# Routed tiles with the up weights held still: VectorE copies each tile's weights, the tokens move, the second transposes go, and the gate is applied to the output

## The reference

```python
scores = jax.nn.sigmoid(xf @ router_w.T)
_, top_idx = jax.lax.top_k(scores + expert_bias, TOP_K)
mask = jax.nn.one_hot(top_idx, N_EXPERTS, dtype=xf.dtype).sum(axis=-2)
gates = scores * mask
h12 = jnp.einsum('td,ehd->teh', xf, w12)
h1, h2 = jnp.split(h12, 2, axis=-1)
h = jax.nn.silu(h1) * h2 * gates[:, :, None]
routed = jnp.einsum('teh,edh->td', h, w3)
```

## Time and profile before

| | |
|---|---|
| median of 3 executions | 1631.92 us |
| the profiled execution, its own time | 1630.51 us |
| its span, as the profiler saw it | 1628.6 us |
| TensorE (PE) matmuls busy | 1590.7 us, 98% of the span |
| VectorE (DVE) busy | 1181.4 us, 73% |
| ScalarE (ACT) busy | 883.4 us, 54% |
| GpSimd (POOL) busy | 732.2 us, 45% |

### The profile page before, as it was taken

The page is one execution under the profiler, slowest core; times in us unless marked ns, Lnnn a source line. Parts: engine busy times, 40 slices in busy tenths (PEclk is TensorE's granted clock), DMA queues, the critical chain, the costliest instruction groups (busy, mean ns, idle before and its releaser), DMA issues.

```text
span 1628.6 us, 42340 instructions
## 1 busy us (share of the span) xinstructions
PE 1590.7 (98%) x15030; PEld 1071.6 (66%) x15031; DVE 1181.4 (73%) x2544; ACT 883.4 (54%) x1528; POOL 732.2 (45%) x676
## 2 busy tenths in 40 slices
PE   7999999999999999999999999999999999998998
PEld 3665566666656776766556666666656777877576
DVE  7777775666667767768866566666788879888876
ACT  5354543444377767764433334444366676674764
POOL 2342242434246566553333323344245567777343
PEclk9999999999999999999999999999999999999999
DMA  7132233333311211003311123333433022221001
GB/s 266 53 106 86 89 105 95 110 110 110 88 40 27 39 26 26 0 2 101 96 36 36 39 72 111 110 108 103 104 66 52 2 80 74 68 61 42 27 26 52
DMA packets 91303, 115.74 MB, mean 71 GB/s; under 512 B 9424, under 2 KB 76528, under 8 KB 91184
## 3 DMA queue, kind: packets, MB, share of 16 engines
q1 hardware_dynamic: 70832, 71.21, 15.0%
q0 software_dynamic: 20352, 42.88, 9.1%
HBM read 66.14 MB, written 47.90 MB: 70 GB/s over the span
## 4 chain that ended last, share of the span: by engine, by line
PE 83%; DVE 7%; issue 3%; ACT 3%; POOL 2%; DMA 1%; DVEq 0%; SPq 0%; ACTq 0%; POOLq 0%
PE ps L2004 19%; PE ps L2006 19%; PE ps L2005 19%; PE ps L2299 3%; PE ps L2298 3%; PE ps L2248 2%; PE ps L2249 2%; PE ps L2020 2%; PE ps L2220 2%; PE ps L2201 2%; PE ps L2538 2%; PE ps L2572 2%; PE ps L2550 1%; PE ps L2400 1%; POOL expert_x L759 1%
## 5 line engine op out<-in xcount | busy, mean ns | idle before, releaser
L787 POOL DMA_INDIRECT routed<-work x142 | 136.1, 959 | 236.4 <-DVE work L1675 231.3
L2004 PE MATMUL ps<-later_hi,work 128*128 (+1 forms) x632 | 202.8, 321 | 0.8 <-ACT work L1019 0.6
L2005 PE MATMUL ps<-later_lo,work 128*128 (+1 forms) x632 | 202.6, 321 | 0.0
L2006 PE MATMUL ps<-later_hi,work 128*128 (+1 forms) x632 | 202.6, 321 | 0.0
L2004 PE MATMUL ps<-xt_hi,wsh 128*128 128x512 f16 x508 | 192.6, 379 | 1.9 <-DVE work L1546 1.3
L2006 PE MATMUL ps<-xt_hi,wsh 128*128 128x512 f16 x508 | 192.5, 379 | 0.0
L2005 PE MATMUL ps<-xt_lo,wsh 128*128 128x512 f16 x508 | 192.5, 379 | 0.0
L975 ACT ACTIVATE work<-ps 128x512 f32<-128x512 f32 x128 | 76.4, 597 | 168.6 <-PE ps L2006 160.5
L1662 DVE SCALAR_TENSOR_TENSOR work<-ps,work 128x256 f32<-128x256 f32 x142 | 68.8, 484 | 99.9 <-ACT work L1026 94.7
L2004 PE MATMUL ps<-wsh,work 128*128 128x256 f16 x512 | 139.5, 273 | 0.7 <-DVE work L1475 0.6
L2005 PE MATMUL ps<-wsh,work 128*128 128x256 f16 x512 | 139.5, 273 | 0.0
(11 more groups left out here) (277 smaller groups left out, 4288.0 us busy)
## 6 DMA issues: line engine op xcount, KB each, us to landing
work<-expert_x SPq DMA_DIRECT2D x142, 129.0 KB
yg<-in_w_later SPq DMA_DIRECT2D x9, 498.0 KB
w1q<-in_w_later SPq DMA_DIRECT2D x9, 498.0 KB
yg<-in_w SPq DMA_DIRECT2D x16, 256.0 KB
values<-wsh SPq DMA_DIRECT2D x8, 512.0 KB, 3.0
later_hi<-values SPq DMA_DIRECT2D x16, 256.0 KB, 3.6
later_lo<-values SPq DMA_DIRECT2D x16, 256.0 KB, 3.4
out_x<-x SPq DMA_DIRECT2D x8, 512.0 KB, 2.9
```

The lines of the kernel that those rows point to most:

```text
L787: nc.gpsimd.indirect_dma_start(routed[:, :], bass.IndirectOffsetOnAxis(m.homes[:, i:i + 1], 0), m.t_y[:, i % 4, :], None).then_inc(s[f"til ...
L2004: nc.tensor.matmul(out_, a[0], b[0], start=start, stop=False)
L2005: nc.tensor.matmul(out_, a[0], b[1], start=False, stop=False)
L2006: return nc.tensor.matmul(out_, a[1], b[0], start=False, stop=stop)
```

## The change

- Before the up product of a tile, VectorE copies its expert's up weights, both halves, 2048 fp16 columns, out of `later` into one of two fixed places (`slots`). VectorE reads the table into a register of its own for this. To let one instruction reach both halves, `later_hi` and `later_lo` become one tensor `later`.
- The up product has the weights still and the tokens moving: 4 parts of 128 hidden units, and for each 2 x 3 matmuls of 128 columns. Its output has hidden units on the partitions.
- So the second transposes (line 2220) go, and `th_hi` and `th_lo` are made from `t_prod` in SBUF.
- The gate belongs to a token, and tokens are no longer on the partitions of `t_prod`; it is applied to the output `t_y`. ScalarE writes it, scaled, to a small tensor `tile_gate` for each tile, and then ScalarE, no longer VectorE, takes `t_y` out of PSUM with it.
- Slot 1 lies on the scratch area where the shared feed-forward keeps `h_hi`, so the copy for tile 1 waits until sequence 6 has finished its down product.

```diff
@@ the slots @@
+            slots = [slot([2, KT, 2 * HE], F16), Carve()([2, KT, 2 * HE], F16)]
@@ ScalarE's round @@
                     if has(0):
                         act.wait_ge(s["tile_turned"], i + 1 + T0)
...
+                        if not isinstance(i, int) or i >= 4:
+                            act.wait_ge(s["tile_y"], i - 3 + T0)
+                        nc.scalar.activation(m.tile_gate[:, u:u + 1], m.tile_x[:, u, D:D + 1], ACT.Copy, scale=0.5 / HS ** 2)
                         nc.scalar.activation(m.t_hi[:, u % 2], ps[:, u % 2, 0:KT * P].rearrange("p (k t) -> p k t", k=KT),
                                              ACT.Copy).then_inc(s["tile_hi"], 1)
+                    if has(2):
+                        j, v = i - 2, u % 2
+                        act.wait_ge(s["tile_prod"], j + 1 + T0)
...
+                        nc.scalar.activation(m.th_hi[:, v], m.t_prod[:, v].rearrange("p (k t) -> p k t", k=EU),
+                                             ACT.Copy).then_inc(s["th_hi"], 1)
                     if has(1):
...
                         nc.scalar.activation(m.t_silu[:, v], ps[:, 2 + v, 0:HE], ACT.Silu, scale=1 / WS).then_inc(s["tile_silu"], 1)
+                    if has(3):
+                        j, v = i - 3, (u - 3) % 4
+                        act.wait_ge(s["tile_down"], j + 1 + T0)
...
+                        nc.scalar.activation(m.t_y[:, v], ps[:, 6 + v % 2, 0:D], ACT.Copy,
+                                             scale=m.tile_gate[:, v:v + 1]).then_inc(s["tile_y"], 1)
@@ VectorE's round @@
+                def weights(i, u):
+
+                    if not isinstance(i, int) or i >= 2:
+                        dve.wait_ge(s["tile_up"], i - 1 + T0)
+                    at = dve.snap(own_columns[u % 2], min_val=0, max_val=(NE - 1) * 2 * HE)
+                    nc.vector.tensor_copy(m.slots[u % 2], up_of[:, :, :, ds(at, 2 * HE)]).then_inc(s["tile_weights"], 1)
+
                 def step(i, b, u, has):
+                    if has(0) and not (isinstance(i, int) and i == 1):
...
+                        weights(i, u)
+                    if has(-1):
+                        dve.load(own_columns[(u + 1) % 2], m.table[0:1, ds(TILES + i + 1, 1)])
...
-                        nc.vector.scalar_tensor_tensor(out=m.t_prod[:, v], in0=ps[:, 2 + v, HE:2 * HE],
-                                                       scalar=m.tile_x[:, (u - 1) % 4, D:D + 1], in1=m.t_silu[:, v],
-                                                       op0=ALU.mult, op1=ALU.mult).then_inc(s["tile_prod"], 1)
...
-                        nc.vector.tensor_scalar(m.t_y[:, v], ps[:, 6 + v % 2, 0:D], 0.5 / (WS * HS), None,
-                                                ALU.mult).then_inc(s["tile_y"], 1)
+                            dve.wait_ge(s["th_lo"], j - 1 + T0)
+                        nc.vector.scalar_tensor_tensor(out=m.t_prod[:, v], in0=ps[:, 2 + v, HE:2 * HE], scalar=HS / WS,
+                                                       in1=m.t_silu[:, v], op0=ALU.mult, op1=ALU.mult).then_inc(s["tile_prod"], 1)
+                    if isinstance(i, int) and i == 1:
+                        dve.wait_ge(s["y_ready"], (NSEQ - 2 + G0) * 2 + 1 + 3)
+                        weights(1, 1)
@@ TensorE's round @@
-                        at = columns(u, 1)
+                        pe.wait_ge(s["tile_weights"], j + 1 + T0)
...
-                        for k in range(KT):
-                            ins = mm3(ps[:, 2 + v, :], (m.t_hi[:, v, k], m.t_lo[:, v, k]),
-                                      both(wup, ds(at + k * NE * 2 * HE, 2 * HE)), k == 0, k == KT - 1)
+                        for part in range(4):
+                            own = slice(part * P, (part + 1) * P)
+                            for k in range(KT):
+                                ins = mm3(ps[:, 2 + v, own], [m.slots[v][:, h, k, own] for h in range(2)],
+                                          (m.t_hi[:, v, k], m.t_lo[:, v, k]), k == 0, k == KT - 1)
...
-                    if has(2):
-                        j, v = i - 2, u % 2
-                        pe.wait_ge(s["tile_prod"], j + 1 + T0)
-                        for k in range(EU):
-                            ins = nc.tensor.transpose(ps[:, 4 + v, k * P:(k + 1) * P], m.t_prod[:, v, k * P:(k + 1) * P], ident)
-                        ins.then_inc(s["th_turned"], 1)
```

54 lines of the change are left out of this document (30 added, 24 removed).

## The result

The changed kernel takes **1622.07 us** (median of 5 runs, 1621.92 to 1622.92) where the kernel before took 1631.21 in the same series (1628.81 to 1631.97): ratio **0.9943 [0.9932, 0.9954]** (in brackets, here and below, the 95% interval). It is faster, by 9 us. The prediction had the sign and nearly every price right, and said 23 us (1631.9 less 1609).

A forecast was written before the change was run, and what follows sets the result against it. TensorE's instruction stream was taken as the bound: 1630.5 us, less 25.6 over 142 tiles, plus 2.6 in the first rounds, gave 1607.5; with the median 1.4 above the profiled run, 1609 us, range 1604 to 1622.

The forecast's parts named there:

- The array's prices: TensorE, each tile: second transposes' 0.22 us removed, up product 1.34 us at 56 ns a matmul, round 2.21 us.
- rival 5: TensorE's up product: pitch nearer 81 ns than 56, 0.64 us more against 0.22 saved, 1694 us; chance 0.02.
- The copy: VectorE's copy of 2048 fp16 weight columns per tile: taken at 0.8 us, costing more than the change saves from 1.14.
- Rival 3: VectorE: slow copy makes it the bound, 1666 us at 1.5 us or 1780 at 2.3; chance 0.05 and 0.02.
- Rival 4: VectorE's copy and GpSimd's row sends get in each other's way, 1655 us; chance 0.05.
- First rounds: Start of each `ffn0`: TensorE waits for VectorE's copies and `t_lo`, 0.3, 0.8 and 0.2 us, 1.3 together.
- The last rounds: End of the tiles: ScalarE's last `t_y` and following work take 2.2 us at most of 2.4 available; costs nothing, barely.
- The step that failed: TensorE's queue: 24 pairs need about 0.44 us of a 2.21 us round, register load 0.31 as before; no bound.
- The cover: VectorE's chain `t_prod`, copy, `t_lo`: ends 2.3 us after its up product, needed at 3.1, 0.8 us to spare.
- Rival 2: ScalarE's round of five activations and three waits binds at some 2.3 us, 1621 us; chance 0.08.

The follow-up runs named there:

- experiment 3: Changed kernel with the loop over groups of four tiles written out on every engine; ratio 0.9884 to the kernel before.
- experiment 1: Changed kernel with ScalarE's gate moved from ahead of `t_hi` to behind it; ratio 0.9895 to the kernel before.
- experiment 10: Changed kernel with two register loads per tile on TensorE, both used, the second for the down product's second half; ratio 1.0120 to the kernel before.
- experiment 12: Changed kernel with the loop written out on all engines and four idle gate copies ahead of `t_hi` on ScalarE; ratio 0.9973 to the kernel before.
- experiment 13: Changed kernel, loop written out on all engines, each up product also waiting for the silu of the tile before; ratio 1.0063 to the kernel before.
- experiment 2: Changed kernel with `t_y` taken one tile later, ahead of silu, and the gate behind it; ratio 0.9907 to the kernel before.
- experiment 4: Changed kernel with VectorE copying 16 instead of 2048 weight columns from tile 2 on; ratio 0.9893 to the kernel before.

## Why the prediction was wrong

*The array's prices* were right: up product 1.34 us at 56 ns a matmul, second transposes gone, round 2.21 us wherever nothing delays it, and for the whole layer in experiment 3. The 81 ns a pair of the Trainium skill ("TensorE: Matmul & The Clock Gate", "Back-to-back issue gap") did not show in 142 up products; the earlier trace rows were the better guide, and rival 5 is out.

*The copy* measured 0.684 us for the 0.8 that I took; the 693 ns of the Trainium skill ("VectorE: DVE Perf Modes", "The perf-mode tier table") agrees. Rival 3 is out.

*Rival 4* is out as I put it: no copy of the changed kernel took more than 0.70 us, so none waited for GpSimd. But the two do get in each other's way. A send that starts 0.1 us into a copy takes 1.41 us, one at 0.3 takes 1.25, one at 0.4 takes 1.08 (medians over the changed kernel's sends), and from 0.6 on, when the copy is nearly over, it takes the 0.96 that it has alone. The other order shows both ways: two sends into which a copy came took 1.44 and 1.46 us, the copy its usual 0.68, and in experiments 1 and 3 a few copies that started while a send ran took up to 0.93. None of this costs time here, as nobody waits for a send. The prediction set aside the rule of the Trainium skill ("SBUF — State Buffer", "Who interferes with whom") by the row at 783.66, where neither operation was longer than usual; these rows agree with it in that the two hold each other up, and not in that the one that comes first always goes free.

*First rounds*: predicted 1.3 us in each layer. The wait for tile 1's copy is 0.7 where 0.8 was said, and the two waits for `t_lo` are 0.3 each where 0.3 and 0.2 were said: 1.3 in all. The rounds say the same: the third and fourth take 2.42 + 2.68 us, before 1.73 + 2.39, and with 0.17 less for each that is 1.3 more than it would be. Right. The last rounds cost nothing visible.

***The step that failed*** is "The register load takes 0.31 us there and is there before as well. The queue is no bound", and with it the round of 2.21 us in the sum. I compared the 0.44 us for 24 pairs with the round, and not the whole of what the queue does in one, from the point at which it may go on, which by experiment 10 is about 2.2 us. The 24 pairs themselves were priced right: the queue passes them in some 0.5 us (303.1 to 303.6 in the round shown). Before, a `t_lo` 1.1 us early let the queue run ahead and all of that was hidden. The change lengthened the queue's part, shortened the array's, and moved `t_lo` to 0.33 us ahead of its use. Of the 13 us that are missing, the rounds hold 10.4 (156.19 and 156.60 against 151.18 twice); by the runs' times experiment 3 brings back 9.6 (0.9943 to 0.9884). The remaining 3 us are not settled. In the changed kernel's profile some 2 us of them lie ahead of the first tile (transposes at 249.03, before at 247.16), where nothing was changed; in the other runs that start lies between 246.85 and 252.68. Almost another 1 is a rounding: the round went from 2.387 to 2.213 us where nothing delays it, 0.174 less and not 0.18, and 142 tiles make 24.7 us of that and not 25.6.

*The cover* was the second half of the same error. I priced the copy's chain at 0.8 us to spare from `t_prod` 0.61 us behind the up product. In the round of the changed kernel shown above `t_prod` starts 1.17 us behind it (first down matmul 300.17, `t_prod` 301.34), as silu was late, and in 51 of 130 rounds `t_lo` waits behind the copy again, for `t_hi`, which I had not put in that chain: `t_hi` stands on ScalarE behind `t_y` and the gate's wait for it.

*Rival 2* (ScalarE's round; 1621 us, chance 0.08) named the right number by luck, and half the cause. Its sum has ScalarE full at 2.3 us a round; ScalarE was busy for 104.5 of 153 us, and experiment 12 gave it 0.4 us more each round, and that hurt by lateness, with idle time left. But the weak point that it named, "the small activation waits for the `t_y` just ahead on its own engine", is real: moving that one activation gave 8 us. Its "against", that silu stands ahead of nothing that TensorE needs in the same round, was wrong, as the queue needs `t_lo`, which comes behind product and copy, long before the array does.

## What to carry to other kernels

- When a change puts more and shorter matmuls into a full TensorE, sum its queue's round as well as the array's: pairs, register loads and operations, waits, branch. And ask how far ahead of the array it runs: take the end of the last operand that it waits for, and the start of the matmul that uses it.
- Busy shares and lists of waits don't show gaps shorter than one matmul's record. Start to start over many rounds does; here a TensorE at 152.5 of 153 us lost 3% (156.2 us for 68 rounds that take 151.2 without delay).
- On an engine that works in order, an operation that waits for its own engine's last result belongs behind those that others wait for.

## What the runs showed that I had not expected

- A loop's branch takes 0.21 us of TensorE's queue (208 ns at the median, 30 times), 45 and 56 ns on ScalarE and VectorE; a register load 0.30 us. With a lead the branch is free (ratio 1.0001 for the kernel before, written out), and so is a second live load in three rounds of four; without one, a live load costs 0.20 us.
- Of two loads into one register one was dropped in the building of the program; an added cost must have a use to be there.
- A row send of GpSimd that starts while a 16-bit copy runs on VectorE takes the longer the earlier it starts (1.41 us at 0.1 us into the copy, 1.25 at 0.3, 0.96 from 0.6 on); a copy that starts while a send runs was 0.68 us in most cases and up to 0.93 in some.
- The end of an up product reached ScalarE either at once or some 0.6 us late: in the changed kernel in 67 of 130 rounds, in experiments 12 and 13 in 126 of 130, in experiments 1 to 4 in none. Its cause is open.
